# Long convolution: the per-channel bias moves into the filter, the gate into the output weights, and the second inverse ahead of the third spectrum

## What is computed

```python
x0, x1, v = (uc[:, :D], uc[:, D:2 * D], uc[:, 2 * D:])
...
k = (h * _decay(t)).T                      # the filter, one row per channel
vx = v * x1
n = 2 * L
y = jnp.fft.irfft(jnp.fft.rfft(vx, n=n) * jnp.fft.rfft(k, n=n), n=n)[..., :L]
v = y + vx * filt_bias[None, :, None]      # bias per channel
yv = (v * x0).transpose(0, 2, 1)
return jnp.einsum('bld,de->ble', yv, out_w) + out_b
...
x = x + ga * _L0_attn_ref(h, ...)          # ga: one gate per batch and column
h = _layernorm(x, axis=-1) * (1 + cb) + sb
```

## Time and profile before

| | |
|---|---|
| runs | 1849.98, 1853.24, 1857.26 us, median 1853.24 |
| the profiled execution | 1850.77 us |
| its span, first to last instruction | 1849.0 us |
| mean granted TensorE clock | 0.977 of full speed |
| busy: PE / DVE / ACT / POOL | 1732.5 / 1420.7 / 1002.2 / 704.2 us |

### The profile page before, as it was taken

The page is one execution under the profiler, slowest core; times in us unless marked ns, Lnnn a source line. Parts: engine busy times, 40 slices in busy tenths (PEclk is TensorE's granted clock), DMA queues, the critical chain, the costliest instruction groups (busy, mean ns, idle before and its releaser), DMA issues.

```text
span 1849.0 us, 27311 instructions
## 1 busy us (share of the span) xinstructions
PE 1732.5 (94%) x9228; PEld 1413.2 (76%) x9228; DVE 1420.7 (77%) x2642; ACT 1002.2 (54%) x2162; POOL 704.2 (38%) x729
## 2 busy tenths in 40 slices
PE   8999799999998789999999979999999897999998
PEld 5878577788877677778887757778888785777887
DVE  6888888875688878887478877887667887888754
ACT  2404477677334356777441537777824245777852
POOL 1141444533241344454234144544323334445332
PEclk8999899999999999999999989999999998999999
DMA  7400534431610064353160044434153006344311
GB/s 287 190 16 1 137 110 132 131 71 47 239 58 0 23 168 119 93 133 81 48 261 1 1 110 136 124 96 115 42 178 125 1 1 177 97 128 131 71 30 52
DMA packets 89103, 183.09 MB, mean 99 GB/s; under 512 B 28991, under 2 KB 42111, under 8 KB 85894
## 3 DMA queue, kind: packets, MB, share of 16 engines
q1 hardware_dynamic: 84512, 169.55, 31.5%
q10 hardware_dynamic: 4454, 11.81, 2.0%
HBM read 124.41 MB, written 46.94 MB: 93 GB/s over the span
## 4 chain that ended last, share of the span: by engine, by line
PE 61%; DVE 16%; issue 7%; ACT 5%; DVEq 3%; DMA 3%; POOL 3%; ACTq 2%; SPq 0%; POOLq 0%
PE ps L452 10%; PE ps L617 7%; PE ps L593 6%; PE ps L622 6%; PE ps L652 5%; PE ps L649 5%; PE ps L647 5%; PE ps L852 4%; PE ps L782 3%; DVE oT L1306 2%; DVE ps L1285 2%; DVE psplit L1295 2%; DVE gT L1413 2%; PE ps L737 2%; PE ps L632 1%
## 5 line engine op out<-in xcount | busy, mean ns | idle before, releaser
L1551 POOL TENSOR_TENSOR psplit<-pT,psplit 128x384 fp32r<-128x384 f32 (+3 forms) x320 | 301.9, 957 | 415.4 <-ACT psplit L991 414.8
L1285 DVE CUSTOM_DVE_ANT_0 ps<-ps,mrow 128x128 f32<-128x128 f32 (+7 forms) x512 | 381.7, 769 | 88.7 <-PE ps L593 85.4
L991 ACT ACTIVATE psplit<-ps 128x512 fp32r<-128x512 f32 (+3 forms) x768 | 373.8, 487 | 0.0
L990 ACT ACTIVATE pT<-ps 128x512 f32<-128x512 f32 (+3 forms) x512 | 256.6, 501 | 140.0 <-PE ps L632 96.1
L617 PE MATMUL ps<-qhh,khl 128*128 128x512 f32 (+3 forms) x768 | 270.3, 352 | 9.0 <-DMA q<-nmr 5.0
L593 PE MATMUL ps<-khl,qhh 128*128 128x512 f32 (+3 forms) x768 | 232.2, 366 | 39.9 <-DMA qhh<-psplit 25.1
L647 PE MATMUL ps<-psplit,vhi 128*65 128x512 f32 (+3 forms) x768 | 264.6, 345 | 0.0
L622 PE MATMUL ps<-q,k 65*128 65x512 f32 (+3 forms) x768 | 260.7, 339 | 0.0
L652 PE MATMUL ps<-psplit,vhi 128*65 128x512 f32 (+3 forms) x768 | 259.7, 338 | 0.0
L649 PE MATMUL ps<-psplit,vlo 128*65 128x512 f32 (+3 forms) x768 | 259.1, 337 | 0.0
L617 PEld LDWEIGHTS ps<-qhh,khl 128*128 128x128 f32 x768 | 144.2, 188 | 59.9 <-DVE mx L1285 11.5
(11 more groups left out here) (215 smaller groups left out, 3288.8 us busy)
## 6 DMA issues: line engine op xcount, KB each, us to landing
qhh<-q_scratch SPq DMA_DIRECT2D x112, 256.0 KB, 5.0
q_scratch<-hrow SPq DMA_DIRECT2D x24, 1024.0 KB, 6.8
mix<-inverse_scratch SPq DMA_DIRECT2D x64, 256.0 KB, 3.5
q<-q_scratch SPq DMA_DIRECT2D x56, 256.0 KB, 4.4
Kf<-kf_scratch SPq DMA_DIRECT2D x3, 3072.0 KB, 17.5
khl<-k_scratch SPq DMA_DIRECT2D x24, 256.0 KB, 7.8
sgn<-sgn_scratch SPq DMA_DIRECT2D x6, 1024.0 KB, 11.0
in_w<-in_w_scratch SPq DMA_DIRECT2D x3, 1536.0 KB, 6.7
```

Source lines behind the costliest of these rows:

```text
L990: A(full(n)[:, 0:hi - lo], ps[:, b, 0:hi - lo], ACT.Exp, scale=SCALE)
L991: A(psplit[:, n % PRING, 0, 0:hi - lo], ps[:, b, 0:hi - lo], ACT.Exp, scale=SCALE)\
L1285: V.tensor_tensor_reduce(out=v, in0=v, in1=mrow[:, L - n:L], scale=1.0, scalar=-3e38, op0=ALU.add, op1=ALU.max, accum_out=mx[:, u % 2, i:i ...
L1551: G.tensor_tensor(psplit[:, n % PRING, 1, 0:m], full(n)[:, 0:m], psplit[:, n % PRING, 0, 0:m].bitcast(F32), ALU.subtract)\
```

## The change

Five things are done together.

1. The bias per channel is added to row 0 (lag 0) of the filter in setup: a new DVE add of 1x256 (`kern[0:1, 0, :] += filt_row`) between the first and the second pair of filter tiles. The bias is loaded as one row, `filt_row`, ahead of `decay`, `fwd` and `fwd_old` in SP's queue; the old load of `filt_b` in columns goes.
2. `skip_and_gate` becomes `gate_rows`: one multiply of the PSUM result with `x0` per dt.
3. The output gate goes into `out_w`: POOL multiplies `out_w` by the gate row once per batch, after the mixing of the gate rows and ahead of its bias adds; `long_out` waits for it (`out_scaled`), and `add_to_x` without a gate adds the PSUM result to `x` directly.
4. On PE `inverse(1)` comes ahead of `spectra(2)`. On DVE the order of the products is new: products (0, 0), (0, 1), (1, 1), then the add into `Yf[1]`, which was POOL's, then (0, 2), (0, 3), (1, 2), (1, 3), `gate_rows(0)`, and the rest.
5. Product (2, 3) goes to the buffer of product (1, 2) in place of PSUM, so spectrum 2's banks are free after it (`re_read` 2). The banks of an inverse are free when its multiply with `x0` is done.

```diff
@@ spectrum_read(j)
-            return at("y_dve", (NB, None, NB + 2, NB + 3)[j])
+            if j == 2:
+                return at("re_read", 2)
+            return at("y_dve", NB + 1 if j == 0 else NB + 3)
@@ buffers
+                    filt_row = sb("filt_row", [1, D], F32, a0)
...
+            made[2, 3] = made[1, 2]
@@ PE
             def inverse(blk):
...
-                if blk == 1:
-                    pe.wait_ge(*at("y_pool", 1))
-                else:
-                    pe.wait_ge(*at("y_dve", (1, None, NB + 1, NB + 3)[blk]))
+                pe.wait_ge(*at("y_dve", (1, 3, NB + 2, NB + 3)[blk]))
                 for dt in range(ND):
                     if u == 0:
-                        bk.take(pe, ("y", ip, dt), at=(6, 0)[ip] + dt)
+                        bk.take(pe, ("y", ip, dt), at=(6, 0)[ip] + dt, until=at("yv_done", ND * ip + dt + 1))
...
                 pe.wait_ge(*at("yv_done", ND * (h + 1)))
+                pe.wait_ge(*at("out_scaled", 1))
...
                 inverse(0)
+                inverse(1)
                 spectra(2)
-                inverse(1)
                 spectra(3)
@@ DVE, setup
             for t in range(0, NT, 2):
                 b = bk.wait(dve, ("kern", t))
+                if t == 2:
+                    dve.drain()
+                    V.tensor_tensor(kern[0:1, 0, :], kern[0:1, 0, :], filt_row[:, :], ALU.add)
@@ DVE, add_to_x
+                    if gate is None:
+                        V.tensor_tensor(x[:, t:t + 2, :], x[:, t:t + 2, :],
+                                        ps[:, b, :].rearrange("p (t n) -> p t n", t=2), ALU.add).then_inc(freed[b], 1)
+                        dve.drain()
+                        stats(x, (t, t + 1))
+                        continue
@@ DVE, after the inverse
-            def skip_and_gate(ip):
+            def gate_rows(ip):
...
-                    V.scalar_tensor_tensor(out=vx[:, dt, cols], in0=vx[:, dt, cols], scalar=filt_b[:, dt:dt + 1],
-                                           in1=ps[:, b, :], op0=ALU.mult, op1=ALU.add).then_inc(freed[b], 1)
-                    dve.drain()
-                    V.tensor_tensor(x0[:, dt, cols], vx[:, dt, cols], x0[:, dt, cols], ALU.mult)\
+                    V.tensor_tensor(x0[:, dt, cols], ps[:, b, :], x0[:, dt, cols], ALU.mult)\
                         .then_inc(s["yv_done"], 1)
@@ DVE, batch
-                for i in range(NB):
+                multiply(0, 0, Yf[0]).then_inc(s["y_dve"], 1)
+                multiply(0, 1, Yf[1]).then_inc(s["y_dve"], 1)
+                multiply(1, 1, made[1, 1]).then_inc(s["prod_done"], 1)
+                dve.drain()
+                V.tensor_tensor(Yf[1], Yf[1], made[1, 1], ALU.add).then_inc(s["y_dve"], 1)
+                for i in (2, 3):
                     multiply(0, i, Yf[i]).then_inc(s["y_dve"], 1)
-                for i in range(1, NB):
+                for i in (2, 3):
                     multiply(1, i, made[1, i]).then_inc(s["prod_done"], 1)
+                gate_rows(0)
+                multiply(2, 2, made[2, 2]).then_inc(s["re_read"], 1)
                 dve.wait_ge(*at("y_pool", 1))
-                multiply(2, 2, made[2, 2]).then_inc(s["re_read"], 1)
-                multiply(2, 3, spectrum(2))
-                skip_and_gate(0)
-                dve.wait_ge(*at("y_pool", 2))
+                multiply(2, 3, made[2, 3]).then_inc(s["re_read"], 1)
                 dve.drain()
                 V.tensor_tensor(Yf[2], Yf[2], made[2, 2], ALU.add).then_inc(s["y_dve"], 1)
                 multiply(3, 3, spectrum(3))
-                dve.wait_ge(*at("y_pool", 3))
-                V.tensor_tensor(Yf[3], Yf[3], spectrum(2), ALU.add).then_inc(s["y_dve"], 1)
+                dve.wait_ge(*at("y_pool", 2))
+                V.tensor_tensor(Yf[3], Yf[3], made[2, 3], ALU.add)
                 dve.drain()
                 V.tensor_tensor(Yf[3], Yf[3], spectrum(3), ALU.add).then_inc(s["y_dve"], 1)
                 dve.wait_ge(*at("gates_mixed", 1))
-                add_to_x("out0", 0, gates[:, 0, :], bias=1)
+                add_to_x("out0", 0, None, bias=1)
                 normed(LN_FFN, 0, x)
-                skip_and_gate(1)
+                gate_rows(1)
                 h_low(LN_FFN, 0)
-                add_to_x("out0", 1, gates[:, 0, :], bias=1)
+                add_to_x("out0", 1, None, bias=1)
@@ POOL, batch
+                if bi:
+                    pool.wait_ge(*at("l0_loaded", 0))
+                G.tensor_tensor(out_w[:, :, :], out_w[:, :, :], gates[:, 0, :].unsqueeze(1).broadcast_to([P, ND, D]),
+                                ALU.mult).then_inc(s["out_scaled"], 1)
                 pool.drain().then_inc(s["gates_mixed"], 1)
...
-                for i in range(1, NB):
+                for i in range(2, NB):
                     pool.wait_ge(*at("prod_done", i))
-                    pool.wait_ge(*at("y_dve", i + 1))
+                    pool.wait_ge(*at("y_dve", i + 2))
                     G.tensor_tensor(Yf[i], Yf[i], made[1, i], ALU.add).then_inc(s["y_pool"], 1)
@@ SP, setup
-            for dst, src in ((decay[:, :, :], d["decay"]), (fwd[:, :, :], d["fwd"][:, 0]),
+            for dst, src in ((filt_row[:, :], d["filt_b"]), (decay[:, :, :], d["decay"]), (fwd[:, :, :], d["fwd"][:, 0]),
                              (fwd_old[:, :, :], d["fwd"][:, 1])):
```

More of the change, by code:

```diff
@@ L78 @@
 LN_FFN, LN_ATT, LN_MOE, LN_NEXT = range(4)
-NLOADED = 11
+NLOADED = 10
 EACH = {"re_done": 4, "pv_done": 192, "tap_done": 12, "vrow_done": 4, "re_copied": 4, "hT_done": 16,
@@ L83 @@
         "q_loaded1": 160, "q2_loaded1": 128, "nmr_done": 16, "exp_done": 192, "o_done": 32, "egelu_done": 8,
-        "mod_picked": 2, "conv_done": 6, "vx_done": 2, "y_dve": 7, "prod_done": 3, "re_read": 1, "yv_done": 4,
+        "mod_picked": 2, "conv_done": 6, "vx_done": 2, "y_dve": 7, "prod_done": 3, "re_read": 2, "yv_done": 4,
         "var_done": 4, "rstd_done": 4, "var_moe": 4, "rstd_moe": 4, "first_hi": 1, "first_lo": 1, "var_next": 1, "rstd_next": 2, "hrow_done": 32, "h_lo_done": 16, "g_lo_done": 16, "rope_a": 20, "rope_done_dve": 1,
         "rope_lo": 10, "nm_done": 16, "low_dve": 80, "inverse_done": 16, "oT_done": 16, "top_done": 1,
-        "w1_split": 2, "x_done": 1, "tap_made": 1, "edge_done": 6, "gates_mixed": 1, "bias_added": 6, "y_pool": 3,
+        "w1_split": 2, "x_done": 1, "tap_made": 1, "edge_done": 6, "gates_mixed": 1, "out_scaled": 1, "bias_added": 6, "y_pool": 2,
         "causal_made": 1, "rope_done": 9, "v_done": 4, "low_pool": 112, "x_loaded": 16,
@@ L150, in adaln_hyena_binffn_gqa_moe @@
         short_b = sb("short_b", [P, INNER // P])
-        filt_b = sb("filt_b", [P, ND])
         tap_b = sb("tap_b", [P, INNER // P])
@@ L318, in adaln_hyena_binffn_gqa_moe @@
                  "mod_picked", "x_loaded", "x_next_loaded", "gates_loaded", "gates_mixed", "var_moe", "rstd_moe", "first_hi", "first_lo", "var_next", "rstd_next", "var_done",
-                 "rstd_done", "hrow_done", "hT_done", "bias_added", "tap_made", "tap_done", "edge_done", "conv_done", "vx_done",
+                 "rstd_done", "hrow_done", "hT_done", "bias_added", "out_scaled", "tap_made", "tap_done", "edge_done", "conv_done", "vx_done",
                  "vrow_done", "prod_done", "y_dve", "y_pool", "yv_done", "gelu_done", "g_lo_done", "h_lo_done",
@@ L537, in _ @@
             gate(1)
-            pe.wait_ge(*at("loaded_windows", 16 * 3))
+            pe.wait_ge(*at("loaded_windows", 16 * 4))
             pe.wait_ge(*at("kern_done", NT // 2))
@@ L1162, in _ @@
             V.tensor_scalar(alpha1[:, :], alpha1[:, :], 1.0 / D, None, ALU.mult)
-            dve.wait_ge(*at("loaded_windows", 16 * 3))
+            dve.wait_ge(*at("loaded_windows", 16 * 4))
             for t in range(0, NT, 2):
                 b = bk.wait(dve, ("kern", t))
+                if t == 2:
+                    dve.drain()
+                    V.tensor_tensor(kern[0:1, 0, :], kern[0:1, 0, :], filt_row[:, :], ALU.add)
                 V.tensor_tensor(kern[:, t:t + 2, :], ps[:, b, :].rearrange("p (t n) -> p t n", t=2),
@@ L1660, in _ @@
                      (br[:, :], d["L1_ffn_br"]), (in_b[:, :], d["in_b"]),
-                     (short_w[:, :, :], d["short_w"]), (short_b[:, :], d["short_b"]), (filt_b[:, :], d["filt_b"]),
+                     (short_w[:, :, :], d["short_w"]), (short_b[:, :], d["short_b"]),
                      (ffn_b1[:, :], d["ffn_b1"]), (rows[:, 0, :], d["L0_attn_out_b"].partition_broadcast(P)),
@@ L1836, in layouts @@
     o["short_b"] = cols(g["L0_attn_short_b"])
-    o["filt_b"] = cols(g["L0_attn_filt_bias"])
+    o["filt_b"] = g["L0_attn_filt_bias"].reshape(1, D)
     o["ffn_b1"] = cols(g["L0_ffn_b1"])
```

## The result

The changed kernel took 1836.26 us (median of 4 runs, 1834.10 to 1836.95) beside 1854.49 for the kernel before (4 runs, 1849.98 to 1857.26): ratio 0.9892, 95% interval 0.9872 to 0.9912. A second set of runs, taken later, gave 1842.25 (5 runs, 1834.18 to 1843.04) beside 1854.29 (20 runs): 0.9931 (0.9907 to 0.9954). The nine times form two groups, five at 1834 to 1837 and four at 1841 to 1843; all nine have 1836.95 in the middle. The gain is 12 to 18 us. The profiled execution took 1836.53, span 1834.7.

The account below looks back on a forecast made before the run. In the long convolution PE and DVE hand work over and late hand-overs decide. Stretches 217.4 become 197.6, plus 0.8 meeting and 1.5 clock, 199.9: gain 17.5 us, from median 1853.24 to 1836; forecast 1829 to 1842, stated range to 1845.

Parts of the forecast that it names:

- (a): Long convolution's products and inverses: second inverse starts at 545.9 against 551.00, worth 5.1 us there; spectrum 2 at 551.15.
- (b): First gating call: 4.75 us, 1.7 of it stall, becomes two 0.61 us multiplies; DVE then idles 1.1 us for spectrum 2.
- (c): Tail of products: DVE gains only 0.6 us, but inverse 2 starts at 561.6 and inverse 3 at 566.95, against 571.10.
- Not what it says: Rival: bank waits still hold inverse 2 until the last add, so (c) gives 0.6, not 4.1; time 1848, chance 0.03.
- half the gain: Rival: DVE loses another 2 us per batch behind spectrum 2, 8 in all; time 1844, chance 0.13.
- (d): Output gate in weights: add_to_x half 3.05 instead of 4.61 us; long_out(1) 4.1 earlier; stretch 48.98 instead of 53.67.
- (e): ACT late next, behind the stretch: its second normalising activations lose 0.42 us per batch again, so 4.27 stays.
- (f): POOL and set-up: DVE's Yf[1] add meets POOL's adds in batch 0, costing 0.8 us (0 to 1.8); set-up add hidden.
- slower rival: POOL's bias adds hold DVE's Yf[1] add in every batch, 6.3 us each; 8 slower, 1861, chance 0.04.
- (g): Clock in the four stretches: slow pieces cost 2.7 us before; half, 1.5, taken as remaining (bounds 0 and 4 x 1.7).
- the sentence of the Trainium skill that I had cited: Clock falls only after long absence of work; new stretches would hold no slow piece, sum 1.5 us better. Prediction trusted rows instead.
- one of the things I said would prove me wrong: Signs of error: stretches over 51.5, a slow clock in all four, or time won coming back in the attention stage.

Follow-up runs that it names:

- e_undo_bias: Changed kernel with the filter's bias applied per channel again behind the inverse, as before; 1858.80 us, ratio 1.0019 to the kernel before.
- e_meet: Changed kernel with POOL's four bias adds waiting until product (0, 1) is made, to meet DVE's add into Yf[1] in every batch; 1842.06 us, ratio 0.9932.
- e_bank_only: Kernel before with only product (2, 3) sent to the buffer of product (1, 2), freeing spectrum 2's banks; 1859.44 us, ratio 1.0032.
- e_undo_order: Changed kernel with the old order of products, inverses and spectra, POOL adding Yf[1] and product (2, 3) in PSUM; 1848.57 us, ratio 0.997.
- e_undo_gate: Changed kernel with the output gate back in add_to_x behind long_out, out_w unscaled; 1855.16 us, ratio 1.0006 to the kernel before.
- e_best2: Changed kernel with half 1's first gate multiply in DVE's rstd wait, plus 20, 6 and 8 extra matmuls in attention-opening waits; 1839.55 us, ratio 0.9909.
- e_best: Changed kernel with half 1's first gate multiply in DVE's rstd wait and 20 extra matmuls at the head of attention; 1832.87 us, ratio 0.9882.
- r_after: The changed kernel itself, unaltered, run again beside its variants on another chip; 1842.25 us, ratio 0.9931 to the kernel before.
- r_undo_gate: Second run, on another chip, of the changed kernel with the output gate applied behind long_out again; 1853.15 us, ratio 0.9986.

## Why the prediction was right, and where it was off

Forecast 1836, measured 1836.26; over both sets of runs 1836.95, in the second alone 1842.25. That the first agrees within 1 us is luck, for two errors of opposite sign are in it. The prediction's sum reaches to the last `h_low` of the second half (ACT's 0.42 a batch lie behind the rows that end a stretch). Up to there the four batches became 20.3 us shorter (236.2 to 215.8) and not 17.5, and the rest of the execution came out worse.

(a) *Products and inverses*: right. On the clock of the earlier trace rows (add 4.16) DVE's add into Yf[1] ends at 545.9, inverse 1 follows inverse 0 without idle (48 matmuls in 10.79), spectrum 2 starts at 551.3 for 551.15.

(b) *Gating*: right. 1.28 us for two multiplies, then 1.14 idle; the 1.7 us stall is gone. e_undo_bias shows that I had put too little on it: I priced the old form by its 4.75 us in the old order, while in the new order it would lose 3.4 us to POOL. The edits are not a sum: undone singly, the order, the bias and the gate cost 3.4, 22.2 and 13.4 us of stretch, 39 together, where all of them win 20.8. The chance I gave to the stage falling short came from spectrum 2 alone.

(c) *Tail of the products*: right within 0.4. Inverse 2 at 561.6 (forecast 561.6), inverse 3 at 567.3 (566.95). The 0.4 is an idle that the trace puts to "issue" before the last add in batch 1; batches 2 and 3 don't lose it and have stretches of 49.06. "Not what it says" is refuted by the PE timeline, "half the gain" by the stretches.

(d) *Gate in the weights*: right. A half takes 3.08 (3.05), `long_out(1)` starts at 575.1 (574.8). Undone alone it costs 13.4 and 12.1 us of stretch in two profiles, for sixteen multiplies with drains at 0.78, 12.5: what the instructions say, with about 1 of the 13.4 by way of the clock.

(e) *ACT late next*: too dark. I charged 4 x 0.42 = 1.7. ACT does start its second normalising set without idle:

```profile
580.20 0.81 ACT L1045 ACTIVATE gfull<-ps,ffn_b,alpha 128x512 f32<-128x512 f32 x1
580.86 0.82 ACT L947 ACTIVATE work<-ps,modb 128x512 f32<-128x512 f32 x1
```

From the second half's rows to the last `h_low` the four batches took 18.7 us before and take 19.2 now, so 0.5 was lost and not 1.7.

(f) *POOL*: the meeting in batch 0 was mis-sized, 0.8 for nothing. The batch has it as foreseen, but it is POOL that pays:

```profile
99.09 6.47 POOL L1548 TENSOR_TENSOR x<-x,mix 128x512 f32<-128x512 f32 x4 [0.19 <-issue]
```

6.47 for the 4.97 of the earlier trace rows, while DVE's add took 1.78. It came at 101.43, as POOL's second add ended (101.59), and so was held for 0.02. That is luck of timing: e_meet's batch 0 shows the hold, 0.21 us. The slower rival stays possible for an operation of DVE that comes in the middle of a POOL add, but DVE gets in at the add's end, so one of POOL's short adds can hold it for 1.24 at most, far from the 4.3 us a batch from which that rival decides. (DVE has three SBUF-only adds in the new order and not four: the last one reads PSUM.) The setup add took 0.41 and stayed hidden.

(g) *Clock*: mis-sized, 1.5 for nothing. No stretch has a slow piece. I had taken half of what the earlier trace rows show as the price. The variants tie it to the waits: it fell behind 2.05 and 1.25 in e_bank_only and 2.23 to 2.58 in e_undo_bias, in every batch, and not behind 1.28 in after. But the length of the wait alone doesn't settle it: of the eight waits of 2.82 in the two profiles without the gate in the weights, four were followed by a fall, and in the kernel before, a wait of 2.32 in batch 1 was not the earlier trace rows.
By the sentence of the Trainium skill that I had cited ("TensorE: Matmul & The Clock Gate", section "HAM oscillation — how this bites in real kernels"), only a long absence of work would do it. Here waits under 3 us did, so the measurement speaks against that sentence, though its number for the new stretches (1.5 better) is the one that came.

*The rest.* I took it as unchanged, and this is the error that cancelled the other. In the two profiles it is 1631.6 and 1638.1, and 5.0 of the 6.5 lie in the opening of attention. The second profile of after has 1635.5, with about 1 more in that opening than before instead of 5.0; the variants go from 1636 to 1647. The kernel before's profile was one of its quicker executions (1850.8, median 1854.5), so the medians say more: the stretches are 20.8 and 20.5 us shorter, the time 18.2 and 12.0, so that 3 us of the stage's gain don't arrive in the first set and 8 in the second. The variants show the same. e_undo_order wins 17.3 in the stretches and 6 to 7 in time, e_undo_gate 7 to 8 and nothing, e_meet 20.6 and 11.4, e_best2 24.5 and 14.7. That it is the opening of attention that takes them (one of the things I said would prove me wrong) isn't shown: two profiles of one kernel differ there by about 4.

What the changed kernel's two groups of times, 6 us apart, come from can be narrowed down. Both of its profiles are of the lower group, but two variants were profiled in a long execution: e_meet (1841.97) and e_best (1840.90, its other three at 1829 to 1834). In both the first spectrum matmul comes late, at 95.9 and 96.1 us, where after has it at 90.9 and r_after at 93.0; that is 5.0 of the 5.5 us between the spans of e_meet and after. It is lost in set-up, where e_meet's code is that of after. Between 25 and 60 us the granted clock is 0.71 in e_meet and e_best and 0.85 in after, and PE's filter matmuls take longer (after, then e_meet):

```profile
36.10 5.25 PE L537 MATMUL ps<-fwo,sine 64*128 64x256 f32 x16
```

```profile
38.65 7.19 PE L537 MATMUL ps<-fwo,sine 64*128 64x256 f32 x16
```

The mean clocks of r_after's runs fit: 0.975 to 0.979 in its four long executions, 0.981 in the short one. So more half clock in set-up can make a difference of this size. What decides on it in an execution stays open, and so does where the rest of the missing gain goes. e_best2, with full clock in the opening and no faster, speaks against the clock there.

## What to carry to other kernels

Price an edit in the order of work in which it will stand: the gate multiplies lost 1.7 us to POOL in the old order and 3.4 in the new one, and edits that shorten the stage by 20 us together shorten it by nothing when one of them is missing. Follow DVE's chain to its end before freeing a bank for PE: e_bank_only removed a 2.3 us wait and got slower. For gains under 1% take two sets of runs and compare variants with the new kernel in the same set; and judge by the stage's stretches, whose sum repeated within 0.3 us for the changed kernel and within 1 for the variant whose clock fell, while the times of one kernel spread over 9.

## What the runs showed of the hardware

A DVE operation and a POOL operation that both have only SBUF operands held each other, and the one that had started first went through. A 0.69 us multiply of DVE that came in the middle of POOL's 128x1536 adds (3.45) took 1.68 and 3.12, until 0.55 us behind their ends. A 128x1536 add of DVE that came as a 128x512 add of POOL (1.24) ended took its 1.76, and POOL's next one took 2.81; coming 0.35 us before that end it took 1.97 (e_meet). A DVE multiply with one operand in PSUM, beside the same long adds, took 0.64. An operation of one SBUF operand is held too: beside a POOL memset of 1x2048 four normalising rows took twice their 1.44 (before the attention: batch 1, where they meet it, batch 0, where they end before it, then POOL in batch 1):

```profile
615.15 3.00 DVE L1191 TENSOR_SCALAR hrow<-x,mv,rstd 128x256 f32<-128x256 f32 x4 [1.12 <-POOL rstd L1528]
```

```profile
176.60 1.44 DVE L1191 TENSOR_SCALAR hrow<-x,mv,rstd 128x256 f32<-128x256 f32 x4 [1.12 <-POOL rstd L1528]
```

```profile
616.19 1.80 POOL L1621 MEMSET k<- 1x2048 f32 x1
```

They met in batches 1 and 3 of after. Whether the 1.6 us are on the path there isn't shown; moving the memset wasn't tried.

The granted clock fell to its lower level, 1.2 GHz, behind short waits of PE: of 2.82 (e_undo_gate, r_undo_gate; four times in eight), of 2.23 to 2.58 (e_undo_bias, four in four), of 2.05 with 1.25 behind it (e_bank_only, four in four), and in e_best2 in the middle of attention after a single wait of 1.70 at 697.5; waits of 1.2 to 1.3, in all four stretches of after, left it at 1.00, and so did one of 2.32. The row of e_best2 behind that wait (length, busy us, granted clock, DMA):

```profile
698.60:701.80 3.20, 3.20 (x13) 2.42 (x12) 0.96 (x5) 1.53 (x4) 1.28 (x2) 0.50 0.02 1
```
